# Key pages kept in two halves in HBM and fetched straight into the score operand, with a two-tensor normalisation

## The chip, the core and the metric

The program runs on one core of one Trainium2 chip. The metric is device time in microseconds (us), from one launch. TensorE (PE in the profile; its weight loads are PEld), VectorE (DVE), ScalarE (ACT), GpSimd (POOL) and SyncE (SP, which here only issues DMAs) run their own instruction streams and meet at semaphores.

## What is computed

A batch of 32 sequences with 32 tokens of 512 features goes through a grouped-query attention block with a paged key and value cache, and then through a dense layer with low-rank experts. Cut to what matters:

```python
q = rope(rmsnorm(x @ Wq.T)); k = rope(rmsnorm(x @ Wk.T)); v = x @ Wv.T      # 32 query heads, 8 key heads, D = 128
k_all = concat(k_cache[block_table], k); v_all = concat(v_cache[block_table], v)   # 16 pages of 32 tokens, + 32 own
scores = where(valid, q . k_all / sqrt(128), -1e30)
x = x + (softmax(scores) . v_all) @ Wo.T
x = x + x @ W.T + 2 * sum_e gate_e * (x @ A_e.T) @ B_e.T                      # top 2 of 8 experts
```

All inputs are float32. Scores and projections are computed in three passes: each operand is split into a high part (rounded to the type fp32r) and a low part (the rest), and hi·hi + hi·lo + lo·hi are summed in PSUM.

## The kernel before

**Tiling.** The eight key heads are taken two at a time: four groups g. In a group the 1024 token rows are eight tiles t of 128 rows (four sequences each), so there are 32 tiles, numbered i = 8g + t. A tile has eight pairs p: sequence b = p // 2 (four of them, ROWS) and key head h = p % 2. Tiles 1 to 5 of a group are one hardware loop, tiles 0, 6 and 7 are written out (walk, L55).

**One pair on each engine.** The orders are written by hand, as the bodies of PE (L632), ACT (L927), DVE (L1196), POOL (L1396) and SP (L419). Each engine takes its instructions in order and stops at each semaphore it waits for.

- PE at pair p: turn_probs(p) transposes the probabilities into PSUM (L576, L577); score(p+2) makes six matmuls of three passes into SX (L556); a piece of the projection of the next tile (proj, at p = 0 to 4); at p = 5 turn_q(i+1, 0) transposes the next queries; weigh(p) multiplies with the values into O (L590, L592). At p = 6 the score is the next tile's first one. project_out, 24 matmuls of 512 columns, starts at p = 7 before weigh(7) and ends the tile.
- DVE at pair p: normalise(p+1) (L1083), minimum(p+2) with the mask (L1076, reading SX), rest_kT(p+3) (L1096), then pieces of rope (rotate, L1052 to L1057), mean_square (L1064), and take_o(p) (L1092), the low part of O, which frees O for the next weigh (o_ready). At the end of a tile split_x (L1040, L1042) splits the input of the tile after the next, and add_y (L1117) adds the output.
- ACT at pair p: take_pT(p) (L842), take_kT(p+3) (L813), four squares with sums at p = 1, 3, 6 (L792), take_qT (L836), exponent(p+2) (L855), next_pages(p) (two DMA issues, L235), fill_slots (L829, the own keys of the tile behind the cached ones), take_block (L781 to L785, the projection out of PSUM), take_o_hi(p) (L849).
- POOL gathers the values of one sequence in four indirect DMAs (L1316), and does the sum, the power and the last product of rope (L1344, L1336, L1355) and the tables (L1331).
- SP issues twelve of the sixteen page fetches of each sequence (L350 to L352), the masks, weights and inputs.

**Pages.** The keys of a group are transposed in eight units of eight pages: PE turns 256 token rows into a PSUM bank (turn_unit, L529), ACT copies the bank to SBUF (take_unit, L761), SP stores it to kT_pages in HBM. Group 0 is turned at the start; the units of group g + 1 are turned during tiles 0 to 6 of group g: unit 0 at (t = 0, p = 2), unit t + 1 at p = 6 (unit_at, L224). A page is fetched as 128 rows of 256 bytes (two heads of 32 tokens, float32) into k_pages. take_kT and rest_kT then split one pair's 512 cached keys into kT, which has four slots; the split of a page is thus made again for every sequence that uses it, 256 times in all.

**Weights.** Each group's weights come in ten halves of 128x1024 through the two buffers of stage. ACT rounds a half (L861) and DVE takes the rest (L1016), at fixed places of tiles 6, 7 and 0 (HI_AT and LO_AT, L239). In tiles 1 to 5 stage is not used.

## Time and profile before

| | us |
|---|---|
| median of 3 runs (1472.35 to 1476.87) | 1476.8 |
| the profiled execution | 1477.62 |
| its span, first to last instruction | 1475.8 |
| start, up to the end of the first tile | 118.7 |
| 15 tiles t = 1 to 5 of groups 0 to 2 (three stretches) | 613.3 |
| 9 tiles t = 6, 7, 0 (three stretches) | 433.0 |
| 5 tiles t = 1 to 5 of group 3 | 193.0 |
| tile 6 of group 3 | 43.0 |
| last tile and the dense layer | 74.8 |

The stretches are bounded by the additions of y at the end of a tile (L1117). A row of the windows view gives for a stretch its length and, for each engine, the time in which it had an instruction running; the granted clock is TensorE's, 1.00 being 2.4 GHz and 0.50 being 1.2 GHz. In a timeline row the bracket is the time for which the engine had nothing to do before this instruction, and what released it. Transfers are 57% of the 16 DMA engines' time in the middle of the run, and 224.33 MB in all.

### The profile page before, as it was taken

The page shows a single profiled execution, that of the slowest core. Times are in us where ns is not written, and L with a number is a line of the kernel's source. Part 1 is how long each engine was busy: PE and PEld are TensorE (multiplying, and loading weights), DVE is VectorE, ACT ScalarE, POOL GpSimd, SP SyncE. Part 2 cuts the span into 40 slices and gives each one's busy share as a digit, 9 for nine tenths or more (in the row PEclk, how much of TensorE's full clock was granted, in tenths as well). Part 3 has the DMA queues.
Part 4 walks back from the last instruction along what each step waited for, and adds up shares of the span by engine and source line. Part 5 has one row for each costly group of instructions (what it writes and reads, how often), then busy time and mean ns, then how long its engine had stood idle before and what let it go on. Part 6 is the DMA issues. An engine that isn't in the chain of part 4 may idle for free. (4 is left out here: it accounts for less than half of the span.)

```text
span 1475.8 us, 34804 instructions
## 1 busy us (share of the span) xinstructions
PE 1255.9 (85%) x8000; PEld 1113.8 (75%) x8000; DVE 942.6 (64%) x2235; ACT 905.1 (61%) x2444; POOL 955.9 (65%) x1136
## 2 busy tenths in 40 slices
PE   4479899888788889889787999889878898999899
PEld 3368888777677778878676888788767787888787
DVE  5466666666756676676566666666676666676754
ACT  4366666666555666665556666666666666666651
POOL 5448776676556777677555876767666777777600
PEclk8689999999999999999999999999999999999999
DMA  8765565555656556555656655555565555555521
GB/s 250 201 171 158 152 154 156 138 153 145 180 155 168 138 148 157 141 154 150 165 139 182 163 145 154 146 146 155 146 178 154 155 142 143 147 140 138 140 77 57
DMA packets 393808, 224.33 MB, mean 152 GB/s; under 512 B 340882, under 2 KB 349362, under 8 KB 393524
## 3 DMA queue, kind: packets, MB, share of 16 engines
q1 hardware_dynamic: 294564, 136.76, 35.6%
q0 software_dynamic: 24576, 67.14, 15.2%
q10 hardware_dynamic: 74544, 19.10, 5.8%
q8 instruction: 38, 0.62, 0.2%
q14 instruction: 86, 0.70, 0.2%
HBM read 204.17 MB, written 20.75 MB: 152 GB/s over the span
## 5 line engine op out<-in xcount | busy, mean ns | idle before, releaser
L1316 POOL DMA_INDIRECT v_rows<-in_kv,step_idx x512 | 524.3, 1024 | 173.4 <-issue 138.3
L855 ACT ACTIVATE soft<-soft,min_all 128x544 f32<-128x544 f32 x256 | 191.6, 749 | 248.5 <-DVE min_all L1076 247.7
L590 PEld LDWEIGHTS O<-pT,v_rows 128*128 128x128 f32 x2048 | 277.8, 202 | 62.6 <-ACT pT L842 44.7
L590 PE MATMUL O<-pT,v_rows 128*128 128x128 f32 x2048 | 290.5, 288 | 38.6 <-DVE oT_lo L1092 27.5
L197 PE MATMUL SX<-kT,qT_hi 128*128 128x288 f32 (+1 forms) x1024 | 226.5, 310 | 56.2 <-ACT kT L829 33.1
L1076 DVE CUSTOM_DVE_ANT_0 soft<-SX,mask 128x544 f32<-128x544 f32 x256 | 183.6, 717 | 96.5 <-PE SX L197 96.2
L1092 DVE TENSOR_TENSOR oT_lo<-O,oT_hi 128x128 fp32r<-128x128 f32 x256 | 73.6, 288 | 241.6 <-ACT oT_hi L849 235.4
L197 PEld LDWEIGHTS SX<-kT,qT_hi 128*128 128x128 f32 x1024 | 164.4, 193 | 75.3 <-issue 51.7
L1336 POOL TENSOR_TENSOR rstd<-meansq,minus_half 128x4 f32<-128x4 f32 (+1 forms) x96 | 101.7, 1060 | 180.3 <-DVE meansq L1064 177.8
L842 ACT ACTIVATE pT<-PT 128x640 f32<-128x640 f32 x256 | 180.7, 706 | 20.7 <-PE PT L577 13.1
L1096 DVE TENSOR_TENSOR kT<-k_pages,kT 128x512 fp32r<-128x512 f32 x256 | 184.4, 721 | 7.0 <-ACT kT L813 3.6
L1083 DVE TENSOR_SCALAR soft<-soft,rden 128x544 f32<-128x544 f32 x256 | 182.8, 714 | 9.1
L197 PE MATMUL PROJ<-w_hi,x_hi 128*128 128x512 f32 x384 | 159.0, 414 | 34.4 <-ACT v_next L783 10.9
L576 PE MATMUL PT<-ident,soft 128*128 128x128 f32 x1024 | 159.2, 279 | 12.6 <-DVE soft L1083 10.7
L813 ACT ACTIVATE kT<-k_pages 128x512 fp32r<-128x512 f32 x256 | 161.9, 632 | 0.0
L197 PE MATMUL PROJ<-w_hi,x_lo 128*128 128x512 f32 x384 | 155.9, 406 | 0.0
L197 PE MATMUL PROJ<-w_lo,x_hi 128*128 128x512 f32 x384 | 154.2, 401 | 0.0
L197 PE MATMUL MISC<-wo_hi,oT_hi 128*128 128x512 f32 x256 | 108.9, 426 | 48.9 <-DVE oT_lo L1092 48.9
L197 PE MATMUL SX<-kT,qT_lo 128*128 128x288 f32 (+1 forms) x512 | 150.1, 293 | 0.0
L576 PEld LDWEIGHTS PT<-ident,soft 128*128 128x128 f32 x1024 | 123.9, 145 | 21.2 <-DVE soft L1083 14.2
L1344 POOL TENSOR_TENSOR rope_u<-rope_u,rope_v 128x512 f32<-128x512 f32 (+1 forms) x94 | 103.8, 1104 | 53.0 <-DVE rope_v L1057 50.7
L849 ACT ACTIVATE oT_hi<-O 128x128 fp32r<-128x128 f32 x256 | 69.6, 272 | 90.8 <-PE O L592 86.0
(222 smaller groups left out, 2382.9 us busy)
## 6 DMA issues: line engine op xcount, KB each, us to landing
k_pages<-kT_pages SPq DMA_DIRECT2D x1536, 32.0 KB
mask<-mask_rows SPq DMA_DIRECT2D x64, 272.0 KB, 3.6
k_pages<-kT_pages ACTq DMA_DIRECT2D x512, 32.0 KB
stage<-in_wqkv SPq DMA_DIRECT2D x22, 512.0 KB, 4.5
x_raw<-in_xT SPq DMA_DIRECT2D x32, 256.0 KB
v_rows<-in_kv,step_idx POOLq DMA_INDIRECT x512
stage<-in_wo SPq DMA_DIRECT2D x16, 512.0 KB, 5.7
y_tile<-y_running SPq DMA_DIRECT2D x32, 256.0 KB
```

Of the source, the lines that this page charges most:

```text
L197: mm = nc.tensor.matmul(out_ps, a, b, start=(c == 0 and k == 0), stop=(c == stop_at and k == 2))
L576: nc.tensor.transpose(PT[:, c * P:(c + 1) * P], probs[:, p % 2, c * P:(c + 1) * P], ident[:, :])
L590: nc.tensor.matmul(O[:, 0:P], v_rows[:, b, c, h * D:(h + 1) * D], pT[:, c * P:(c + 1) * P], start=c == 0, stop=False)
L813: nc.scalar.activation(kT[:, p % SLOTS, 0, 0:L].rearrange("p (j s) -> p j s", s=PSIZE), k_pages[:, b, :, h, :], ACT.Copy).then_inc(sm["kT_ ...
L842: nc.scalar.activation(pT[:, :], PT[:, 0:L + P], ACT.Copy).then_inc(sm["pT_ready"], 1)
L855: nc.scalar.activation(probs[:, p % 2, 0:KEYS], scores[:, p % 2, :], ACT.Exp, bias=min_all[:, p:p + 1], scale=-1.0, accum_out=den[:, p:p + ...
L1076: V.tensor_tensor_reduce(scores[:, p % 2, :], SX[:, SX_AT:SX_AT + KEYS], mask[:, b, :], 1.0, BIG, ALU.add, ALU.min, min_all[:, p:p + 1]).t ...
L1083: V.tensor_scalar(probs[:, p % 2, 0:KEYS], probs[:, p % 2, 0:KEYS], rden[:, p:p + 1], None, ALU.mult).then_inc(sm["probs_ready"], 1)
L1096: V.tensor_tensor(kT[:, p % SLOTS, 1, 0:L].rearrange("p (j s) -> p j s", s=PSIZE), k_pages[:, p // GK, :, p % GK, :], kT[:, p % SLOTS, 0, ...
L1316: G.indirect_dma_start(v_rows[:, b, c, :], None, v_half[:, :], bass.IndirectOffsetOnAxis(ap=step_idx[:, b * LC + c:b * LC + c + 1], axis=0 ...
L1336: G.tensor_tensor(rstd[:, 0:n], meansq[:, k, 0:n], minus_half[:, 0:n], ALU.pow).then_inc(sm["pow_ready"], 1)
L1344: G.tensor_tensor(rope_u[:, 0:w], rope_u[:, 0:w], rope_v[:, 0:w], ALU.add).then_inc(sm["sum_ready"], 1)
```

## The change

- A page in kT_pages is now 128 rows of 512 bytes: high parts of both heads, then low parts (PAGE_BYTES doubles). The split is made once for each unit: take_unit on ACT writes the high part, the new rest_unit on DVE the low part (32 times each), and the store writes both. take_kT and rest_kT (256 times each) are gone.
- kT holds all 16 pages of four sequences and the own keys behind them; a fetch writes into it directly. PE's score waits for the page DMAs (kp_in) where it waited for kT_ready, and a fetch into kT waits until the last score that reads those pages is done (s_done) where it waited for kT_ready. The moving operand of a score is now runs of 32 columns, 512 bytes apart; before it was 288 or 256 columns in one piece.
- The units of the next group are turned in tiles 1 to 4, two in each, at p = 2 and p = 6, in the stage buffers that the weights don't use then. The hardware loop (walk_tiles) is over tiles 1 to 4; tile 5 is written out. The first two halves of the next weights are loaded at tile 5.
- normalise multiplies by the broadcast reciprocal as a second tensor instead of a scalar operand, and mean_square takes its epsilon from a tensor.
- On ACT next_pages comes directly after take_pT, ahead of squares and exponential; take_unit comes after take_o_hi. On PE turn_q(i+1, 0) comes ahead of score at p = 5. On DVE split_x moves from the end of the tile to p = 6.
- At the start all eight units are turned before the first projection, their loads come first, and the first fetches of ACT stand later. The running y of the last layer lies in v_rows and q_rot.

The core of the diff:

```diff
-    PAGE_BYTES = D * GK * PSIZE * 4
+    PAGE_BYTES = D * 2 * GK * PSIZE * 4
     U8 = mybir.dt.uint8
-    kT_dram = nc.dram_tensor("kT_pages", (GROUPS * PAGES, D, GK * PSIZE), F32, kind="Internal").ap()
+    kT_dram = nc.dram_tensor("kT_pages", (GROUPS * PAGES, D, 2 * GK * PSIZE), F32, kind="Internal").ap()
...
-        k_pages = sb("k_pages", [P, ROWS, NPP, GK, PSIZE])
-        kn = sb("kn", [P, 2, GK * D])
+        kT = sb("kT", [P, ROWS, NPP + 1, 2, GK, PSIZE], F32R)
+        k_new = sb("k_new", [P, ROWS, 2, GK, SEQ], F32R)
...
-        kT = sb("kT", [P, SLOTS, 2, KEYS], F32R)
-        k_new = sb("k_new", [P, ROWS, GK, 2, SEQ], F32R)
...
+        kn = [stage[:, 0, k, :].rearrange("p (c n) -> p c n", c=2) for k in range(2)]
+
+        def unit_views(ps, dst):
+            src = ps.rearrange("p (h q s) -> p h q s", h=GK, q=UNIT_PAGES)
+            return src, [dst[:, :, z, :, :].rearrange("p q h s -> p h q s") for z in range(2)]
...
+        def unit_split(u, startup):
+            w = (wo_hi if u < 4 else wo_lo)[:, 2 * (u % 4):2 * (u % 4) + 2, :] if startup else stage[:, 1, :, :].bitcast(F32R)
+            return w.rearrange("p a n -> p (a n)").rearrange("p (q z h s) -> p q z h s", q=UNIT_PAGES, z=2, h=GK)
...
+        UNIT_AT = (2, 6)
...
+            return 2 * t - 2 + UNIT_AT.index(p)
...
-                sp.wait_ge(sm["kT_ready"], (i - 1) * PAIRS + b * GK + GK)
+                sp.wait_ge(sm["s_done"], (i - 1) * PAIRS + b * GK + GK)
...
+            def load_kn(n, g, u, k):
+
+                if k == 0:
+                    sp.wait_ge(sm["w_lo_ready"], g * HALVES)
+                    sp.nop(nofuse=True)
+                sp.wait_ge(sm["ku_done"], n - 1)
                 sp.nop(nofuse=True)
-                sp.dma_start(kn[:, :, :], kv[bass.ds(g * TOKENS_CACHED + u * (2 * P), 2 * P), 0:GK * D]
-                             .rearrange("(c p) n -> p c n", p=P)).then_inc(sm["kn_in"], 16)
+                sp.dma_start(kn[k], kv[bass.ds(g * TOKENS_CACHED + u * (2 * P), 2 * P), 0:GK * D]
+                             .rearrange("(c p) n -> p c n", p=P)).then_inc(kn_in[k], 16)
...
+            for c in range(4):
+                sp.dma_start(v_rows[:, c, :, :], kv[c * 4 * P:(c + 1) * 4 * P, 0:GK * D].rearrange("(c p) n -> p c n", p=P)
+                             ).then_inc(kn0_in[c], 16)
...
+                turning = not final and not fixed
...
+                if turning:
+                    for k in range(2):
+                        load_kn(n_unit + 2 * t - 2 + k, g + 1, 2 * t - 2 + k, k)
...
+                        sp.wait_ge(sm["ku_stored"], (g + 2) * 16 * UNITS)
+                        sp.nop(nofuse=True)
+                        next_half(g + 1, 0)
...
-                pe.wait_ge(sm["kT_ready"], n + 1)
+                if h == 0:
+                    pe.wait_ge(kp_in[b], (i + 1) * 16 * NPP)
...
-                    k_hi, k_lo = (kT[:, p % SLOTS, z, j0:j1] for z in range(2))
-                    mm = three_pass(SX[:, SX_AT + j0:SX_AT + j1], lambda c: (q_hi, q_lo), lambda c: (k_hi, k_lo), 1, 0, 0)
+                    k_hi, k_lo = (kT[:, b, j0:j1, z, h, :] for z in range(2))
+                    mm = three_pass(SX[:, SX_AT + j0 * SEQ:SX_AT + j1 * SEQ], lambda c: (q_hi, q_lo), lambda c: (k_hi, k_lo), 1, 0, 0)
...
+                    if not last and p == 5:
+                        turn_q(i + 1, 0)
...
-                    if not last and p == 5:
-                        turn_q(i + 1, 0)
...
-                nc.scalar.activation(unit_turned(u, startup).rearrange("p q h s -> p h q s"), unit_view(ps), ACT.Copy
-                                     ).then_inc(sm["ku_ready"], 1)
+                src, (hi, lo) = unit_views(ps, unit_split(u, startup))
+                nc.scalar.activation(hi, src, ACT.Copy).then_inc(sm["ku_hi"], 1)
...
-            def take_kT(i, p):
-                b, h = p // GK, p % GK
-                n = i * PAIRS + p
-                if h == 0:
-                    act.wait_ge(kp_in[b], (i + 1) * 16 * NPP)
-                if not (isinstance(n, int) and n < SLOTS):
-                    act.wait_ge(sm["min_ready"], CREDIT + n - SLOTS + 1)
-                nc.scalar.activation(kT[:, p % SLOTS, 0, 0:L].rearrange("p (j s) -> p j s", s=PSIZE), k_pages[:, b, :, h, :],
-                                     ACT.Copy).then_inc(sm["kT_hi_ready"], 1)
...
-                if not (isinstance(n, int) and n == 0):
-                    act.wait_ge(sm["s_done"], n)
-                nc.scalar.activation(kT[:, :, :, L:KEYS],
-                                     k_new[:, 2 * half:2 * half + 2, :, :, :].rearrange("p b h z s -> p (b h) z s"), ACT.Copy
+                if not (isinstance(i, int) and i == 0):
+                    act.wait_ge(sm["s_done"], (i - 1) * PAIRS + (half + 1) * (PAIRS // 2))
...
-                        act.wait_ge(sm["kT_ready"], i * PAIRS + p + GK)
+                        act.wait_ge(sm["s_done"], i * PAIRS + p + GK)
...
-                    if p + 3 < PAIRS:
-                        take_kT(i, p + 3)
-                    elif not last:
-                        take_kT(i + 1, p + 3 - PAIRS)
+                    if not last:
+                        next_pages(p)
...
-                    if not last:
-                        next_pages(p)
-                    u = unit_at(t, p)
-                    if u is not None and not final:
-                        take_unit(UNITS + g * UNITS + u, u, KT[:, :], False)
...
+                    u = unit_at(t, p)
+                    if u is not None and not final:
+                        take_unit(UNITS + g * UNITS + u, u, KT[:, :], False)
...
-                V.tensor_scalar(meansq[:, k, 0:n], sumsq[:, k, 0:n], 1.0 / D, EPS, ALU.mult, ALU.add
-                                ).then_inc(sm["ms_ready"], 1)
+                V.scalar_tensor_tensor(meansq[:, k, 0:n], sumsq[:, k, 0:n], 1.0 / D, eps[:, 0:n], ALU.mult, ALU.add
+                                       ).then_inc(sm["ms_ready"], 1)
...
-                V.tensor_scalar(probs[:, p % 2, 0:KEYS], probs[:, p % 2, 0:KEYS], rden[:, p:p + 1], None, ALU.mult
+                V.tensor_tensor(probs[:, p % 2, 0:KEYS], probs[:, p % 2, 0:KEYS], rden[:, p:p + 1].to_broadcast([P, KEYS]), ALU.mult
...
-            def rest_kT(i, p):
-                dve.wait_ge(sm["kT_hi_ready"], i * PAIRS + p + 1)
-                V.tensor_tensor(kT[:, p % SLOTS, 1, 0:L].rearrange("p (j s) -> p j s", s=PSIZE), k_pages[:, p // GK, :, p % GK, :],
-                                kT[:, p % SLOTS, 0, 0:L].rearrange("p (j s) -> p j s", s=PSIZE).bitcast(F32), ALU.subtract
-                                ).then_inc(sm["kT_ready"], 1)
+            def rest_unit(n, u, ps, startup):
+                dve.wait_ge(sm["ku_hi"], n + 1)
+                src, (hi, lo) = unit_views(ps, unit_split(u, startup))
+                V.tensor_tensor(lo, src, hi.bitcast(F32), ALU.subtract).then_inc(sm["ku_ready"], 1)
...
-                    if p + 3 < PAIRS:
-                        rest_kT(i, p + 3)
-                    elif not last:
-                        rest_kT(i + 1, p + 3 - PAIRS)
...
+                    u = unit_at(t, p)
+                    if u is not None and not final:
+                        rest_unit(UNITS + g * UNITS + u, u, KT[:, :], False)
...
+                        if not (final and fixed and t >= TILES - 2):
+                            split_x(i + 2)
...
-                if not (final and fixed and t >= TILES - 2):
-                    split_x(i + 2)
```

The order of instructions on ACT in the loop over tiles, pair 5. Before:

```order
L842 ACTIVATE pT<-PT 128x640
L810 REGISTER_ALU
L812 ISA
L813 ACTIVATE kT<-k_pages 128x512
L834 REGISTER_ALU
L836 ACTIVATE qT_hi<-MISC 128x4x4x32
L854 REGISTER_ALU
L855 ACTIVATE soft,den<-soft,min_all 128x544
L235 DMA k_pages<-kT_pages 128x256 x2
L829 ACTIVATE kT<-k_new 128x8x32
L849 ACTIVATE oT_hi<-O 128x4x32
```

Now:

```order
L858 ACTIVATE pT<-PT 128x640
L256 DMA kT<-kT_pages 128x512 x2
L850 REGISTER_ALU
L852 ACTIVATE qT_hi<-MISC 128x4x4x32
L870 REGISTER_ALU
L871 ACTIVATE soft,den<-soft,min_all 128x544
L845 ACTIVATE kT<-k_new 128x2x128
L865 ACTIVATE oT_hi<-O 128x4x32
```

The high part of the keys (L813 before) is gone, the two fetches stand directly behind pT, and the exponential is followed at once by the own keys (kT<-k_new) that the next score needs.

DVE in the same loop, from the minimum at pair 6 on. Before:

```order
L1076 ISA soft,min_all<-SX,mask 128x544
L1076 ISA min_all 128x1
L1095 REGISTER_ALU
L1096 TENSOR_TENSOR kT<-k_pages,kT 128x512
L1092 TENSOR_TENSOR oT_lo<-O,oT_hi 128x4x32
L1064 TENSOR_SCALAR meansq<-sumsq 128x4
L1081 RECIPROCAL rden<-den 128x1
L1083 TENSOR_SCALAR soft<-soft,rden 128x544
L1095 REGISTER_ALU
L1096 TENSOR_TENSOR kT<-k_pages,kT 128x512
L1092 TENSOR_TENSOR oT_lo<-O,oT_hi 128x4x32
```

Now:

```order
L1099 TENSOR_TENSOR oT_lo<-O,oT_hi 128x4x32
L1102 ISA
L1104 TENSOR_TENSOR stage<-KT,stage 128x2x8x32
L1071 SCALAR_TENSOR_TENSOR meansq<-sumsq,eps 128x4
L1044 ISA
L1046 REGISTER_ALU
L1047 CAST x_hi<-x_raw 128x512
L1049 TENSOR_TENSOR x_lo<-x_raw,x_hi 128x512
L1087 REGISTER_ALU
L1088 RECIPROCAL rden<-den 128x1
L1090 TENSOR_TENSOR soft<-soft,rden 128x544
L1099 TENSOR_TENSOR oT_lo<-O,oT_hi 128x4x32
```

The low part of the keys (L1096 before) is gone at both pairs; the low part of a unit (stage<-KT) and the split of x now stand between the low part of O and the next normalisation.

PE in the same loop, pair 5. Before:

```order
L576 MATMUL PT<-ident,soft 128x128 x4
L577 MATMUL PT<-ident,soft 128x128
L563 REGISTER_ALU
L197 MATMUL SX<-kT,qT_hi 128x288 x2
L197 MATMUL SX<-kT,qT_lo 128x288
L197 MATMUL SX<-kT,qT_hi 128x256 x2
L197 MATMUL SX<-kT,qT_lo 128x256
L550 MATMUL MISC<-ident,q_rot 128x128 x4
L590 MATMUL O<-pT,v_rows 128x128 x4
L592 MATMUL O<-pT,v_own 128x128
```

Now:

```order
L607 MATMUL PT<-ident,soft 128x128 x4
L608 MATMUL PT<-ident,soft 128x128
L580 MATMUL MISC<-ident,q_rot 128x128 x4
L596 REGISTER_ALU
L199 MATMUL SX<-kT,qT_hi 128x288 x2
L199 MATMUL SX<-kT,qT_lo 128x288
L199 MATMUL SX<-kT,qT_hi 128x256 x2
L199 MATMUL SX<-kT,qT_lo 128x256
L621 MATMUL O<-pT,v_rows 128x128 x4
L623 MATMUL O<-pT,v_own 128x128
```

The four transposes of the next queries have moved ahead of the six score matmuls.

## Rows read from the trace of the kernel before

**Rows 1.** The page: busy time and share of each engine.

```profile
PE 1255.9 (85%) x8000; PEld 1113.8 (75%) x8000; DVE 942.6 (64%) x2235; ACT 905.1 (61%) x2444; POOL 955.9 (65%) x1136
```

**Rows 2.** Windows: PE, PEld, DVE, ACT, POOL busy (instructions), granted clock, DMA share, GB/s.

```profile
0.00:118.70 118.70, 69.70 (x343) 58.38 (x344) 64.04 (x136) 57.33 (x140) 62.03 (x81) 0.83 0.74 205
118.70:323.00 204.30, 182.90 (x1212) 164.69 (x1211) 133.76 (x331) 133.32 (x370) 150.71 (x181) 0.97 0.57 149
323.00:469.00 146.00, 118.47 (x733) 103.13 (x732) 94.42 (x210) 88.56 (x233) 88.05 (x103) 0.95 0.61 163
469.00:674.00 205.00, 184.18 (x1209) 165.98 (x1208) 132.52 (x330) 132.87 (x370) 149.06 (x181) 0.97 0.57 148
674.00:821.00 147.00, 119.03 (x734) 103.76 (x733) 95.20 (x210) 88.93 (x233) 90.53 (x103) 0.94 0.60 162
821.00:1025.00 204.00, 183.91 (x1207) 165.31 (x1205) 131.03 (x330) 132.55 (x370) 146.65 (x179) 0.97 0.56 149
1025.00:1165.00 140.00, 116.36 (x722) 101.72 (x720) 94.66 (x209) 87.91 (x231) 89.35 (x102) 0.95 0.60 161
1165.00:1358.00 193.00, 175.17 (x1190) 158.26 (x1190) 131.41 (x331) 130.56 (x365) 147.03 (x176) 1.00 0.55 144
```

**Rows 3.** Lines L813, L1096, L1083, L765: duration ns min/median/max.

```profile
L813 ACT ACTIVATE kT<-k_pages x256: 613/630/657, 50.7 to 1413.9; 128x512 fp32r<-128x512 f32 x128
...
L1096 DVE TENSOR_TENSOR kT<-k_pages,kT x256: 678/686/2235, 51.6 to 1414.9; 128x512 fp32r<-128x512 f32 x128
...
L1083 DVE TENSOR_SCALAR soft<-soft,rden x256: 502/504/2133, 56.3 to 1419.2; 128x544 f32<-128x544 f32 x128
...
L765 ACT ACTIVATE kn<-KT x24: 597/597/598, 86.1 to 1060.0; 128x512 f32<-128x512 f32 x24
```

**Rows 4.** Waits of TensorE, whole span: us in total, times, longest.

```profile
PE MISC L197 <- DVE oT_lo L1092: 48.9, 28, 2.6
PE SX L197 <- ACT kT L829: 33.1, 34, 1.7
PE O L590 <- DVE oT_lo L1092: 27.5, 26, 1.5
```

**Rows 5.** Timeline of one tile of the last group: start us, us, what [idle before].

```profile
1265.43 1.13 PE L590 MATMUL O<-pT,v_rows 128*128 128x128 f32 x8 [0.69 <-DVE oT_lo L1092]
...
1267.77 0.42 ACT L829 ACTIVATE kT<-k_new 128x256 fp32r<-128x256 f32 x1 [0.35 <-issue]
...
1268.53 0.50 PE L197 MATMUL SX<-kT,qT_hi 128*128 128x288 f32 x2 [1.19 <-ACT kT L829]
...
1268.78 1.39 DVE L1083 TENSOR_SCALAR soft<-soft,rden 128x544 f32<-128x544 f32 x1
...
1271.89 0.28 ACT L849 ACTIVATE oT_hi<-O 128x128 fp32r<-128x128 f32 x1 [0.21 <-issue]
...
1272.64 0.47 PE L197 MATMUL MISC<-wo_hi,oT_hi 128*128 128x512 f32 x1 [1.47 <-DVE oT_lo L1092]
```

**Rows 6.** Timeline of TensorE at the same place, tile of another group.

```profile
1014.99 0.47 PE L197 MATMUL MISC<-wo_hi,oT_hi 128*128 128x512 f32 x1 [2.36 <-DVE oT_lo L1092]
...
1016.08 0.63 PE L197 MATMUL MISC<-wo_lo,oT_hi 128*128 128x512 f32 x1
```

**Rows 7.** Timeline around a group boundary.

```profile
721.05 0.49 PE L197 MATMUL PROJ<-w_hi,x_hi 128*128 128x512 f32 x1 [2.72 <-DVE x_lo L1042]
...
749.13 2.13 DVE L1083 TENSOR_SCALAR soft<-soft,rden 128x544 f32<-128x544 f32 x1
```

**Rows 8.** The page: DMA queues, packets, MB, share of 16 engines.

```profile
q0 software_dynamic: 24576, 67.14, 15.2%
q10 hardware_dynamic: 74544, 19.10, 5.8%
```

**Rows 9.** Timeline of the start.

```profile
48.91 0.60 ACT L785 ACTIVATE raw<-PROJ 128x512 f32<-128x512 f32 x1 [6.22 <-issue]
...
52.58 0.82 PE L197 MATMUL SX<-kT,qT_hi 128*128 128x288 f32 x2 [10.52 <-DVE kT L1096]
```

154 lines of the change are left out of this document (73 added, 81 removed).

## The prediction

> **What bounds the kernel now.** I read the page first: TensorE has a matmul running for 85% of the span, VectorE, ScalarE and GpSimd for 61 to 65% [rows 1]. So TensorE sets the time, together with whatever makes it wait, and the next question is where it waits. I cut the span at the ends of tiles [rows 2]. In the last group five tiles take 193.0 us, 38.6 each, at full clock. In the other groups five such tiles take 204 to 205, 41 each, at a granted clock of 0.97. Three tiles around a group boundary, where the weights are split, take 140 to 147, 48 each, at 0.94 to 0.95: TensorE is busy for 119.0 of 147.0 us there. The start takes 118.7.
>
> The list of TensorE's waits names the handovers: for the low part of O on VectorE before project_out (48.9 us, 28 times) and before weigh (27.5), for the own keys from ScalarE (33.1) [rows 4]. None is long by itself. In one tile of the last group they are three gaps [rows 5]: A, 0.69 us before weigh(5); B, 1.19 before the next tile's first score; C, 1.47 before project_out. That is 3.35 us, so the tile without gaps would take 38.6 - 3.35 = 35.3 us. In the other groups gap C is 2.36 us, since a unit's copy (0.6 us) stands ahead of the high part of O, and behind it matmuls of 512 columns take 0.63 instead of 0.39 to 0.40: the granted clock has gone from 2.4 to 1.2 GHz [rows 2, 6].
>
> All three gaps end a chain that runs over both ScalarE and VectorE, each of which works through a fixed order. What is taken out of these orders shortens the chain; what is taken out elsewhere is worth nothing.
>
> **Part 1: the split of pages.** It removes 256 x 0.63 = 161 us from ScalarE and 256 x 0.72 = 184 from VectorE (the median there is 0.686) [rows 3], and adds 32 copies of about 0.6 and 32 differences of about 0.69: net 142 and 162 us. None of it is TensorE's, so it counts only through the gaps. For a tile without a unit:
>
> - Gap A waits for take_o(4), behind rope's last block, behind ScalarE's copy of it. Both engines lose one key half ahead of it (0.63 and 0.69), and the copy no longer stands behind two fetches (0.35 us of issue time, as before the own keys in rows 5). TensorE comes there about 0.5 later, as turn_q now lies in front. Gap A goes: 0.69.
> - Gap B waits for fill_slots behind exponent(7). By the same chain it starts about 1.0 earlier, but TensorE comes 0.69 earlier. Net 0.3 gained: about 0.9 stays.
> - Gap C waits for take_o(6), at the end of pT, two fetches, four squares and the exponential on ScalarE. 0.63 goes, but the exponential needs minimum(0) of the next tile, which stands behind a normalisation that took 1.39 us [rows 5]. I take half of it: net 0.3 gained, 1.2 stays.
>
> Together 1.3 us a tile. Five tiles of the last group: 6.5 us.
>
> **Part 2: units in tiles 1 to 4.** Two units a tile where there was one. Each costs TensorE four transposes, at most 4 x 1.13 / 8 = 0.56 us; I take 0.5. The one at p = 6 falls into gap B and costs nothing, the one at p = 2 costs 0.5. ScalarE's copy now comes behind the high part of O, so gap C is that of the last group and I expect the clock to stay at 2.4 GHz as it did there. VectorE's difference (0.69) now stands before mean_square at p = 6; GpSimd's power and product come after that, and turn_q(i+1, 1) needs them: I take 0.6 for it (between nothing, if rope's chain has slack, and 1.2, if x's split in front of the next normalisation counts too). A tile is then 38.6 - 1.3 + 0.5 + 0.6 = 38.4, and tile 5, without units, 37.3. Twelve and three of these are 460.8 + 111.9 = 572.7 us against 613.3 [rows 2]: 40.6 us.
>
> **Part 3: group boundaries.** TensorE idles for 28 of 147 us there; three tiles without weights idle for 3 x 3.5 = 11 [rows 2], so 17 are the boundary's. The split of x moves from behind a weight half to p = 6, and its wait of 2.72 us [rows 7] goes. Three units leave (1.5 us of transposes). A clock of 0.94 on 147 us is up to 8.8 us lost; I give back 3 with the long wait. Of the other 14 us idle I take half, 7, since the engines that split weights lose 15 and 17 of their 89 and 95 us. 14.2 us a boundary, 42.6 for three. The last group's tile 6 and last tile: 2.5 together, by the same share.
>
> **Part 4: normalisation.** Its median is 504 ns, but its longest 2133 [rows 3, 7]; its mean is 714. The nearest row for the new form is L1096, also a product of two SBUF tensors: 686 ns at 512 columns, so 729 at 544, with a longest of 2235. In total nothing changes (729 against 714 x 256), if the stalls go; if they all stay, 210 ns each, VectorE gains 58 us of work. I take a third of them. The Trainium skill, "SBUF — State Buffer", section "SBUF: two separate sides", says that a VectorE operation with two SBUF inputs still takes the port pair it shares with GpSimd, but only against a GpSimd operation that reads SBUF. By that rule stalls behind gathers would end and those behind rope's sums (1.39 us in rows 5 is one, with L1344 beside it in the trace) would stay, which speaks against a full gain; the sum above already leaves gap C for that.
>
> **Part 5: transfers.** A page row grows from 256 to 512 bytes, 2048 x 128 = 262,144 packets. A packet of ScalarE's queue, 256 bytes, takes 5.8% x 16 x 1475.8 / 74,544 = 18.4 ns, one of GpSimd's, 2732 bytes on average, 146 [rows 8]. On a line between them 512 bytes take 31.6. The extra is between nothing and 18.4 ns a packet, or 0 to 301 us of all 16 engines; I take 13.1 ns, 215 us. The DMA share goes from 0.57 to about 0.75: busy, not full. Fetches start up to seven pairs ahead, so in the loop I cost this at nothing; what it costs if that cover is gone is rival 4. ("DMA: Bandwidth & Descriptors" in the Trainium skill, section "Specifications", names 512 bytes as the least transfer for line rate; by that rule the extra would be near nothing. No row here has such packets in number.)
>
> **Part 6: the start.** The third projection's copy stood 6.22 us behind fetches, and the first score waited 10.52 us [rows 9]. Both now come earlier; then twelve fetches (some 6.5 us) stand before the first exponential instead. I take 7 us off, for the first scores and for the page list that all wait for. The bound on the other side: 64 fetches and 8 stores, 16,384 packets, are 13.4 us more of all engines at 13.1 ns, at a share of 0.74 already [rows 2]; not hidden, the start is 6 us longer than now.
>
> **The sum.** 6.5 + 40.6 + 42.6 + 2.5 + 7 = 99.2 us. From the profiled execution, 1477.6 (span 1475.8), this gives 1378.4; the median of the three runs is 0.8 lower, so 1378.
>
> **Rivals.**
>
> 1. *The chains fall wholly behind TensorE.* For: only 3.35 us a tile is idle, and both engines lose a fifth of their work. Against: squares, exponential and own keys still follow each other within 3.8 us. A further 2.1 us in 20 tiles and 7 at each boundary: 1378 - 63 = 1315.
> 2. *The two-input product stalls as the old one did.* VectorE carries 58 us more, at the pairs where the chain runs. Then B and C keep their length (-12), units cost a further 1 us in twelve tiles (-12), and boundaries gain half (-21): 1378 + 45 = 1423.
> 3. *TensorE reads 32-column runs more slowly: slower than before.* No moving operand of the old trace was in pieces. A pair's scores are 3 x 544 = 1632 columns, 0.68 us at 2.4 GHz; at half rate 256 pairs add 174 us, all on TensorE: 1552. It turns the result from 57% longer on (99 of 174). Against: the copies of ScalarE and VectorE read such pieces without a loss (L813, 630 ns for 512 columns, against 597 for L765) [rows 3].
> 4. *Pages come late.* The score now waits for the DMA itself, two pairs later than the split did, but nothing buffers it. SP issues twelve fetches in 6 us, and the last sequence's pages can only be asked for after pair 7's score. At 2 us a tile: 1378 + 64 = 1442; from 3.1 us a tile on nothing is gained.
>
> That the new order does not do what it says (fetches ahead of the exponential cost ScalarE the same 0.35 us, only elsewhere) lies within the forecast, since squares follow them directly at three pairs.
>
> **Chances.** Forecast (1350 to 1410) 0.55; rival 1 0.17; rival 2 0.15; rival 3 0.06; rival 4 0.07. The range 1320 to 1440 leaves out rival 3, a third of rival 1 and half of rival 4, some 0.16. A measurement of this kernel tells 0.3% from no change. Faster by more than that 0.91, the same 0.02 (the far end of rival 4), slower 0.07.
>
> **What would show it.** Tiles 1 to 5 of the last group at 37.3 us each, with gap A gone, B near 0.9 and C near 1.2; the same tiles of other groups at 38.4 with the clock at 1.00; the boundary stretches at 130; score matmuls of 256 and 288 columns as long as before; no wait of the scores for kT_pages; normalisations at about 729 ns with a few above 1.2 us; a DMA share of 0.65 to 0.8. The prediction is wrong if scores wait for DMAs, if the boundaries keep their 145 us, or if GpSimd, whose gathers and rope work fill 147 of 193 us [rows 2] and leave little room, becomes what TensorE waits for.

## The result and the profile after

The changed kernel takes 1431.1 us (median of 4 runs, 1428.3 to 1434.3) against 1476.8: a ratio of 0.970, 95% interval 0.967 to 0.973. It is faster by 46 us; 99 were forecast. The profiled execution took 1432.97 us, its span is 1431.1. Between the two profiled spans TensorE's idle time fell by 18 us (span less busy time, 219.9 to 201.5) and its busy time by 26 (1255.9 to 1229.6, the same 8000 matmuls, at a granted clock of 0.973 instead of 0.957).

The busy line of the page, the granted clock and the DMA share of the changed kernel:

```profile
PE 1229.6 (86%) x8000; PEld 1091.1 (76%) x8000; DVE 837.2 (58%) x2012; ACT 770.8 (54%) x2188; POOL 956.4 (67%) x1136
...
PEclk8689999999999999999999999999999999999999
DMA  8877777777767777877767777777777676777711
```

Against [rows 1], ScalarE and VectorE have lost work, as the change meant; TensorE's share has hardly risen. The windows view, bounded by the ends of tiles as in [rows 2]: length, busy us of each engine, granted clock, DMA share and GB/s.

```profile
0.00:118.00 118.00, 66.26 (x331) 55.00 (x332) 60.95 (x134) 49.30 (x125) 60.64 (x80) 0.80 0.78 240
118.00:318.70 200.70, 181.13 (x1225) 162.45 (x1224) 121.44 (x299) 113.70 (x334) 146.77 (x177) 1.00 0.78 222
318.70:455.00 136.30, 113.77 (x716) 99.86 (x715) 79.11 (x184) 73.98 (x206) 92.75 (x105) 0.96 0.73 210
...
656.60:791.70 135.10, 110.88 (x716) 97.41 (x715) 79.81 (x185) 73.51 (x206) 93.64 (x107) 0.97 0.73 211
...
992.10:1124.10 132.00, 111.63 (x717) 98.35 (x716) 80.08 (x185) 73.89 (x206) 94.45 (x107) 0.97 0.74 216
1124.10:1312.10 188.00, 175.92 (x1192) 158.88 (x1191) 113.84 (x290) 111.10 (x326) 143.22 (x177) 1.00 0.73 204
```

Put beside the forecast (spans, us; "four waits gone" is run e17 below):

| stretch | before | forecast | changed | four waits gone |
|---|---|---|---|---|
| start and first tile | 118.7 | 111.7 | 118.0 | 106.3 |
| 15 tiles t = 1 to 5, groups 0 to 2 | 613.3 | 572.7 | 602.7 | 582.0 |
| 9 tiles t = 6, 7, 0 | 433.0 | 390.4 | 403.4 | 376.7 |
| 5 tiles t = 1 to 5, group 3 | 193.0 | 186.5 | 188.0 | 185.6 |
| the rest | 117.8 | 115.3 | 119.0 | 116.6 |

The last group came out nearly as forecast. The missing time lies in the start (6 us), the 15 tiles of groups 0 to 2 (30), the boundaries (13) and the rest (4). TensorE's waits in the changed kernel (total us, times, longest) name the places; the answer to [rows 4]:

```profile
PE MISC L199 <- DVE oT_lo L1099: 37.0, 32, 1.3
PE SX L199 <- ACT kT L845: 27.9, 35, 1.1
PE O L621 <- ACT pT L858: 26.2, 13, 5.2
PE PROJ L580 <- POOL q_rot L1360: 13.9, 20, 0.9
PE PROJ L199 <- ACT raw L811: 11.9, 5, 10.4
...
PE PROJ L199 <- ACT v_next L809: 10.7, 2, 9.9
...
PE KT L563 <- DMA stage<-in_kv: 7.5, 7, 2.2
```

The first two are the old gaps C and B. The other five are new or grown, each with one place in an order behind it (v_next had 10.9 us before too, but its longest was 4.8). Four of them (the probabilities pT, the queries q_rot, v_next and KT) are taken away in e17; the one for raw, 10.4 us in the start, is not touched by any experiment.

**The start.** Timeline of the changed kernel, first tile:

```profile
67.52 0.85 SPq L332 DMA_DIRECT2D stage<-in_wo  x2
...
68.54 6.54 SPq L256 DMA_DIRECT2D kT<-kT_pages  x12
...
75.13 0.31 SPq L358 DMA_DIRECT2D pages<-page_bytes  x1
...
78.75 0.87 ACTq L256 DMA_DIRECT2D kT<-kT_pages  x2
...
79.73 0.75 ACT L871 ACTIVATE soft<-soft,min_all 128x544 f32<-128x544 f32 x1 [14.68 <-issue]
...
81.24 0.79 PE L199 MATMUL PROJ<-w_hi,x_hi 128*128 128x512 f32 x1 [9.86 <-ACT v_next L809]
```

ScalarE's next fetches need the second tile's page list (pages), which SP loads behind all 48 fetches of the first tile. They stood behind the exponential before; now the exponential stands behind them, for 14.68 us, and TensorE waits 9.86 for what follows it.

Earlier in the start stands the wait for raw, in the same timeline:

```profile
33.84 0.85 SPq L332 DMA_DIRECT2D stage<-in_wqkv  x2
...
37.91 1.06 ACT L904 ACTIVATE w_hi<-stage 128x1024 fp32r<-128x1024 f32 x1 [10.68 <-DMA stage<-in_wqkv]
...
40.73 0.79 PE L199 MATMUL PROJ<-w_hi,x_hi 128*128 128x512 f32 x1 [10.39 <-ACT raw L811]
...
53.12 0.82 PE L199 MATMUL SX<-kT,qT_hi 128*128 128x288 f32 x2 [5.88 <-DMA kT<-kT_pages]
```

SP issues these two weight halves behind the stores of the units, at 33.84 us; before, it issued them at 25.36, and the same wait of TensorE was 3.39 us. So the first score comes at 53.12 us, no earlier than before (52.58 in [rows 9]).

**Tile 7.** Timeline of the changed kernel, group 1, pairs 2 and 3:

```profile
710.90 4.15 SPq L256 DMA_DIRECT2D kT<-kT_pages  x7
...
715.37 0.33 SPq L332 DMA_DIRECT2D stage<-in_wqkv  x1
...
720.39 1.06 ACT L877 ACTIVATE w_hi<-stage 128x1024 fp32r<-128x1024 f32 x1 [7.81 <-DMA stage<-in_wqkv]
...
721.35 0.69 ACT L858 ACTIVATE pT<-PT 128x640 f32<-128x640 f32 x1
722.09 1.23 PE L621 MATMUL O<-pT,v_rows 128*128 128x128 f32 x4 [5.20 <-ACT pT L858]
```

SP issues the weight half behind twelve page fetches, as in the kernel before. But by the records ScalarE now comes to it 12.6 us after the addition that ends the last tile (before, 15.5), and SP issues it after 15.4 (14.1 and 14.3 in the other two groups; before, 12.6 to 13.0). ScalarE stands 7.81 us at it, and TensorE waits 5.20 for the probabilities behind it. The three boundaries have such a wait each, 4.8 us in the mean.

**Pair 6 of a tile with a unit**, timeline of the changed kernel (group 2, t = 1):

```profile
862.60 0.29 DVE L1099 TENSOR_TENSOR oT_lo<-O,oT_hi 128x128 fp32r<-128x128 f32 x1 [1.07 <-ACT oT_hi L865]
...
863.09 0.69 DVE L1104 TENSOR_TENSOR stage<-KT,stage 128x512 fp32r<-128x512 f32 x1 [0.20 <-ACT stage L792]
863.69 0.15 DVE L1071 SCALAR_TENSOR_TENSOR meansq<-sumsq,eps 128x4 f32<-128x4 f32 x1
...
863.93 1.16 POOL L1341 TENSOR_TENSOR rstd<-meansq,minus_half 128x4 f32<-128x4 f32 x1 [3.63 <-DVE meansq L1071]
...
865.22 1.42 POOL L1360 TENSOR_TENSOR q_rot<-rope_u,rstd 128x512 f32<-128x512 f32 x1
...
866.69 0.55 PE L580 MATMUL PROJ<-ident,q_rot 128*128 128x128 f32 x3 [0.92 <-POOL q_rot L1360]
```

The mean square (0.15 us of work) waits behind the unit's copy on ScalarE and difference on VectorE; GpSimd has been idle for 3.63 us, and TensorE for 0.92 us before it turns the queries.

### The profile page after: what moved, and what is told of

Read it like the earlier page. It is cut to its first block and busy times, and to the rows that moved or that the text cites. A ratio compares the mean times of both kernels' runs of the same rounds, so it can differ in the third digit from the quotient of the medians.

```text
span 1431.1 us, 33847 instructions
## 1 busy us (share of the span) xinstructions
PE 1229.6 (86%) x8000; PEld 1091.1 (76%) x8000; DVE 837.2 (58%) x2012; ACT 770.8 (54%) x2188; POOL 956.4 (67%) x1136
## 3 DMA queue, kind: packets, MB, share of 16 engines
q10 hardware_dynamic: 74544, 35.88, 8.9%
## 5 line engine op out<-in xcount | busy, mean ns | idle before, releaser
L621 PE MATMUL O<-pT,v_rows 128*128 128x128 f32 x2048 | 279.0, 280 | 38.3 <-ACT pT L858 26.2
L621 PEld LDWEIGHTS O<-pT,v_rows 128*128 128x128 f32 x2048 | 264.8, 194 | 61.1 <-ACT pT L858 36.1
L1083 DVE CUSTOM_DVE_ANT_0 soft<-SX,mask 128x544 f32<-128x544 f32 x256 | 183.8, 718 | 93.4 <-PE SX L199 92.5
L1090 DVE TENSOR_TENSOR soft<-soft,rden 128x544 f32<-128x544 f32 x256 | 230.9, 902 | 8.8
L199 PE MATMUL PROJ<-w_hi,x_hi 128*128 128x512 f32 x384 | 155.8, 406 | 31.0 <-ACT raw L811 11.9
L199 PE MATMUL MISC<-wo_hi,oT_hi 128*128 128x512 f32 x256 | 105.4, 412 | 37.0 <-DVE oT_lo L1099 37.0
L1349 POOL TENSOR_TENSOR rope_u<-rope_u,rope_v 128x512 f32<-128x512 f32 (+1 forms) x94 | 107.9, 1148 | 21.9 <-DVE rope_v L1064 20.0
L1059 DVE TENSOR_TENSOR rope_u<-raw,table 128x512 f32<-128x512 f32 (+1 forms) x96 | 57.9, 603 | 100.0 <-ACT raw L811 65.7
L199 PEld LDWEIGHTS PROJ<-w_hi,x_hi 128*128 128x128 f32 x384 | 74.5, 194 | 45.6 <-issue 15.7
```

Source lines behind the costliest of these rows:

```text
L199: mm = nc.tensor.matmul(out_ps, a, b, start=(c == 0 and k == 0), stop=(c == stop_at and k == 2))
L621: nc.tensor.matmul(O[:, 0:P], v_rows[:, b, c, h * D:(h + 1) * D], pT[:, c * P:(c + 1) * P], start=c == 0, stop=False)
L1083: V.tensor_tensor_reduce(scores[:, p % 2, :], SX[:, SX_AT:SX_AT + KEYS], mask[:, b, :], 1.0, BIG, ALU.add, ALU.min, min_all[:, p:p + 1]).t ...
L1090: V.tensor_tensor(probs[:, p % 2, 0:KEYS], probs[:, p % 2, 0:KEYS], rden[:, p:p + 1].to_broadcast([P, KEYS]), ALU.mult).then_inc(sm["probs ...
L1349: G.tensor_tensor(rope_u[:, 0:w], rope_u[:, 0:w], rope_v[:, 0:w], ALU.add).then_inc(sm["sum_ready"], 1)
```

## The experiments

e1 to e8, e17 and e18 are told against 1431; the kernel before, which ran beside each, took 1475 to 1477 us there. In the sessions of e9 to e16 it took 1560 to 1562 us, with VectorE and ScalarE idle for reasons that the trace doesn't name, so these are compared with each other only. An interval behind a time is that of the ratio to the kernel before.

**e1: the page list early, at the start.**

```diff
+                if b == 2:
+                    sp.wait_ge(sm["pages_read"], 1)
+                    sp.nop(nofuse=True)
+                    load_list(1)
                 for j in range(SP_PAGES):
                     fetch_page(sp, b, j, page[b % 2 * SP_PAGES + j])
...
-            sp.wait_ge(sm["pages_read"], 1)
-            load_list(1)
```

> At the start SyncE loads the second tile's page list before it issues the fetches of the third and fourth sequence, not after them. Theory (a few new order slots ate the gain): the 9.9 us for which TensorE waits in the first tile, while ScalarE holds its next exponential back for the list, go almost wholly: 8 to 10 us off the changed kernel, 1422. The first tile ends at 109 instead of 118 us. Rival (the start is bound by transfers, at a DMA share of 0.78): the wait moves to the pages of sequences 2 and 3, gain under 3 us, 1429.

Measured 1429.3 (ratio 0.963 to 0.971): 2 us, too little to tell from nothing (four runs of 1428.6 to 1430.2 against 1428.3 to 1434.3). The wait of 9.9 us is gone from the trace, but later in the first tile stands one of 6.9, "PE O <- ACT pT": the next in the order of the same queue, a weight half behind twelve page fetches, at which ScalarE stands 7.0 us. The theory named the wait rightly and its worth wrongly; the rival's time fits, its reason doesn't (see e3).

**e2: the weight half ahead of the fetches, in tile 7.**

```diff
+                if ending:
+                    next_half(g + 1, 5)
                 if not last:
                     read_pages(i + 1, 0)
                     load_pages(i + 1, 0)
...
-                if ending:
-                    next_half(g + 1, 5)
```

> In the last tile of groups 0 to 2 SyncE issues the sixth weight half ahead of the first twelve page fetches, not behind them. Theory (order): the half is issued 9 us earlier and has landed when ScalarE comes to it; TensorE's wait of 4.8 us before weigh(3) goes in three tiles: 14 us off, 1417, boundary stretches at 128 to 131. Rival (512-byte packets fill the queues, so that what is issued also lands later): the half's transfer grows and the pages of sequence 0 come late instead, gain under 5 us, 1427.

Measured 1415.3 (0.954 to 0.963): 16 us, where the theory said 14. The first boundary stretch of it, in the windows view:

```profile
315.90:445.90 130.00, 111.36 (x716) 98.44 (x715) 79.36 (x184) 73.72 (x206) 91.30 (x106) 0.97 0.75 220
```

**e3: half the bytes.** A fetch takes `[:, 0:GK * PSIZE * 4]` of each row, 256 bytes, and k_lo is read from the high part, so the low part of the keys is left out of the result.

> A fetch takes only the high parts, 256 bytes a row, and the score uses the high part of the keys twice, so the low part of the keys is left out of the result; matmuls, orders and packet counts stay. The share of the DMA engines falls to that of the kernel before. Theory (bytes are hidden, order slots are not): the waits for the page list (9.9) and for the weight half (4.8 a boundary) stay within 1 us; only the wait for the unit's rows (0.84 in 9 tiles) shrinks: 1420 to 1430. Rival (bytes): waits for transfers go everywhere, 1390 to 1405.

Measured 1425.2 (0.961 to 0.969): 6 us for 67 MB less, at the edge of the noise (the changed kernel's interval is 0.967 to 0.973). Averaged from the records, the start's wait goes from 9.9 to 7.5 us, tile 7's from 4.8 to 3.7, that for a unit's rows from 0.84 to 0.79. So the bytes lengthen these waits a little, the order makes them.

**e4: the scalar normalisation**, in the changed kernel.

```diff
-                V.tensor_tensor(probs[:, p % 2, 0:KEYS], probs[:, p % 2, 0:KEYS], rden[:, p:p + 1].to_broadcast([P, KEYS]), ALU.mult
+                V.tensor_scalar(probs[:, p % 2, 0:KEYS], probs[:, p % 2, 0:KEYS], rden[:, p:p + 1], None, ALU.mult
```

> Only the normalisation goes back to the scalar operand. Theory: its median falls from 725 to 504 ns and its mean from 902 to about 720, 47 us less of VectorE, of which gaps B and C give 0.2 us each a tile: 10 us off, 1421. Rival (the chain through VectorE is what keeps the gaps): 0.7 us and more a tile, 1405 or less. Second rival (the scalar form blocks GpSimd, which now works 67% of the time and has TensorE waiting for q_rot): no gain or slower, 1430 to 1438.

Measured 1412.4 (0.953 to 0.961): 19 us off, between the theory's 10 and the rival's 26. **e5** is the mirror, the tensor form in the kernel before:

> The kernel before, with only the normalisation by a second tensor. Theory (the new form costs VectorE 0.2 us a normalisation, and stalls behind rope's sums as the old one did): the mirror of what undoing it gave in the changed kernel (19 us): 1477 + 10 to 19 = 1487 to 1496. Rival (it paid in the kernel before, where 22 normalisations stalled beside gathers, and costs only since the orders changed): 1470 to 1477.

Measured 1502.4, 1.018 (1.016 to 1.021) of the kernel before: 27 us slower than the kernel before beside it, past the theory's range. Durations (minimum/median/longest, ns) of the normalisation in the changed kernel, in e4 and in e5:

```profile
L1090 DVE TENSOR_TENSOR soft<-soft,rden x256: 724/725/2491, 57.1 to 1374.7; 128x544 f32<-128x544 f32 x128
```

```profile
L1090 DVE TENSOR_SCALAR soft<-soft,rden x256: 502/504/2166, 56.5 to 1352.5; 128x544 f32<-128x544 f32 x128
```

```profile
L1083 DVE TENSOR_TENSOR soft<-soft,rden x256: 724/726/2415, 57.7 to 1443.0; 128x544 f32<-128x544 f32 x128
```

The median rises by 0.22 us and the longest stay. In both kernels this part of the change cost time. In e5 the clock hid some of it; windows view, the first five tiles and those of the last group:

```profile
121.70:326.50 204.80, 179.93 (x1212) 160.52 (x1211) 145.84 (x332) 133.13 (x370) 153.88 (x176) 1.00 0.58 149
1179.10:1379.70 200.60, 177.58 (x1192) 158.17 (x1191) 144.90 (x331) 130.25 (x366) 153.06 (x176) 1.00 0.55 138
```

The last group takes 200.6 instead of 193.0 [rows 2], 1.5 us a tile. The first stretch takes 204.8, as before, but at a clock of 1.00 instead of 0.97: gap C is 2.0 us there instead of 2.3 (averages from the records), and the matmuls behind it run at 2.4 GHz (in the 15 tiles 2 of project_out's 360 take over 550 ns, in the kernel before 38).

**e6: mean_square ahead of take_o and rest_unit** at pair 6.

```diff
+                    if not last and p == 6:
+                        mean_square(i + 1, 2)
                     take_o(i, p)
...
-                        mean_square(i + 1, 2)
```

> In the changed kernel mean_square of pair 6 stands ahead of take_o and rest_unit on VectorE. Theory (in the tiles with units GpSimd's power and product wait behind the copy, the low part of O and the unit's difference): TensorE's 0.92 us before turn_q(i+1, 1) go in 12 tiles and 0.3 in others: 12 to 15 us off, 1417; unit tiles 39.8. Rival (the squares of ScalarE end no earlier, and VectorE now waits for them ahead of the low part of O): nothing gained, gap C grows, 1431 to 1436.

Measured 1408.2 (0.953 to 0.959): 23 us, more than the theory's 15. "PE PROJ <- POOL q_rot" (13.9 us, 20 times) is no longer among the waits of TensorE. Five tiles of the first group, in its windows view:

```profile
114.20:310.00 195.80, 179.82 (x1225) 162.40 (x1224) 118.80 (x299) 113.38 (x334) 144.05 (x176) 1.00 0.80 226
```

195.8 instead of 200.7. By the records tiles 2 to 4 gain 0.9 us each, tile 1 0.7 and tile 5 1.5, where a wait for q_rot before MISC goes too. The wait for a unit's rows grows meanwhile, from 0.84 to 1.27 in tiles 2 to 4.

**e7: own keys and the high part of O ahead of the exponential** (ScalarE, pairs 5 and 6).

```diff
+                    if not last and p == 5:
+                        fill_slots(i + 1, 0)
+                    if p == 6:
+                        take_o_hi(i, p)
                     if p + 2 < PAIRS:
                         exponent(i, p + 2)
...
-                    if not last and p == 5:
-                        fill_slots(i + 1, 0)
...
-                    take_o_hi(i, p)
+                    if p != 6:
+                        take_o_hi(i, p)
```

> In the changed kernel ScalarE takes the own keys (pair 5) and the high part of O (pair 6) ahead of the exponential, in the 0.6 and 0.9 us in which it waits for the minimum. Theory (gaps B and C are places in ScalarE's order, not its load): B falls from 0.89 to under 0.3 and C from 1.30 to about 0.5, some 1.2 us a tile in 29 tiles: 35 us off, 1396. Rival (VectorE's and GpSimd's part of the chain ends at the same time): under 0.4 us a tile, 1420.

Measured 1413.2 (0.955 to 0.959): 18 us, half of the theory's 35. Gaps B and C fall to 0.2 us and less, as the theory said or further, and in tiles with units too. In the last group a tile gains 1.2 us, but in tiles with units nothing: there TensorE's wait for q_rot grows from 0.9 to 1.6 and that for the unit's rows from 0.84 to 1.25. By the stretches 10 of the 18 us come from the boundaries and 6 from the last group. A gap is worth what the next chain leaves.

**e8: all of it together**: e1, e2, e4, e6, e7 and the two further edits that stand at e17.

> The changed kernel with all of it: page list early, the weight halves of tiles 7 and 0 ahead of page fetches, mean_square early, the rows of the units asked for first in a tile, the scalar normalisation, own keys and high part of O ahead of the exponential. Theory (each wait was its own): 19 + 8 + 18 + 12 + 10 + 35 = 102 us off 1431, 1329, with 5 to 15 us given back where one wait hid another: 1329 to 1344. Rival (the gain of each was another's cover): over 1375.

Measured 1357.2 (0.916 to 0.922): 74 us off, between theory and rival, the fastest kernel of this study. Alone e4 and e7 gave 19 and 18 us; added to e17 (below) they give 13 together. Its busy line:

```profile
PE 1227.7 (90%) x8000; PEld 1090.3 (80%) x8000; DVE 791.0 (58%) x2012; ACT 770.8 (57%) x2188; POOL 913.9 (67%) x1136
```

**e17: the four new waits taken away, nothing else.** It is e1, e2 and e6, the weight halves of tile 0 in the same way, and the units' rows asked for first in a tile; normalisation and ScalarE's order stay as changed. What it adds to e1, e2 and e6:

```diff
+                if turning:
+                    for k in range(2):
+                        load_kn(n_unit + 2 * t - 2 + k, g + 1, 2 * t - 2 + k, k)
                 if not (final and fixed and t >= TILES - 2):
                     load_x(i + 2, (t + 2) % TILES if fixed else t + 2)
...
-                if turning:
-                    for k in range(2):
-                        load_kn(n_unit + 2 * t - 2 + k, g + 1, 2 * t - 2 + k, k)
...
+                if ending:
+                    next_half(g + 1, 5)
+                if fixed and t == 0:
+                    next_half(g, WO_FIRST + 2)
                 if not last:
                     read_pages(i + 1, 0)
                     load_pages(i + 1, 0)
                 if fixed and t == 0:
-                    next_half(g, WO_FIRST + 2)
-                if ending:
-                    next_half(g + 1, 5)
+                    next_half(g, WO_FIRST + 3)
```

> The kernel of e11 and e14, the changed kernel without its four new waits. Theory: 55 us off 1431, 1376 to 1384, a ratio of 0.932 to 0.937 to the kernel before. Rival (a chain through VectorE with the slower normalisation takes the place of each wait): 1395 or more, 0.945.

Measured 1370.3 (0.924 to 0.932): 61 us off the changed kernel. Its stretches, windows view:

```profile
0.00:106.30 106.30, 63.41 (x330) 52.96 (x331) 61.23 (x133) 49.78 (x125) 61.98 (x84) 0.87 0.86 264
106.30:300.70 194.40, 180.10 (x1225) 162.53 (x1223) 122.73 (x298) 114.02 (x334) 143.61 (x176) 1.00 0.80 231
300.70:428.30 127.60, 109.63 (x716) 96.73 (x715) 81.36 (x184) 73.72 (x206) 89.93 (x107) 0.99 0.77 224
1049.40:1235.00 185.60, 173.64 (x1185) 158.07 (x1185) 117.58 (x293) 112.69 (x328) 143.62 (x176) 1.00 0.73 207
```

Alone e1, e2 and e6 give 2 + 16 + 23 = 41 us, so 20 come from the two further edits and from taking the waits away together; no run tells these apart. Against the profiled execution of the changed kernel TensorE's idle time falls by 44 us (201.5 to 157.4) and its busy time by 20 (1229.6 to 1209.9), at a granted clock of 0.988 instead of 0.973. What e8 gains beyond e17 its boundaries give back in part: by the records the 15 tiles fall from 582.0 to 569.1 us and the last five from 185.6 to 180.8, but the three boundaries rise from 376.7 to 385.5, at a clock of 0.95, 0.99 and 0.95 where e17 has 0.99, 0.99 and 1.00.

**e18: e8_all with the page list ahead of the fetches of sequence 2** in every tile.

```diff
                     read_pages(i + 1, 1)
+                    if not (final and fixed and t == TILES - 2):
+                        sp.wait_ge(sm["pages_read"], i + 2)
+                        sp.nop(nofuse=True)
+                        load_list(i + 2)
                     load_pages(i + 1, 2)
...
                     load_pages(i + 1, 3)
-                    if not (final and fixed and t == TILES - 2):
-                        sp.wait_ge(sm["pages_read"], i + 2)
-                        sp.nop(nofuse=True)
-                        load_list(i + 2)
```

> The kernel of e8_all with one edit: in every tile SyncE loads the next page list ahead of the fetches of sequence 2, not behind those of sequence 3. Theory (ScalarE stands up to 5 us at the page list at pair 0, TensorE 0.9 us at pair 1 in tiles 2 to 4 and 2.6 in tile 7): 16 off 1357, 1338 to 1346, a ratio of 0.91. Rival (the wait moves to the gathers of GpSimd or to the weights): 1352 or more.

Measured 1368.5 (0.924 to 0.930), 11 us slower than e8_all: the rival. ScalarE's idle "issue" time before exponentials falls from 92.9 to 6.8 us, so the list was what it waited for, and TensorE's waits for v_next fall from 22.9 to 1.7; but ScalarE's waits for weight halves rise from 8.5 to 30.1 us, and TensorE's for pT from 11.2 to 34.3 and for a unit's rows from 8.3 to 14.5. Why these transfers land later isn't settled.

**e9 to e16, the other sessions.** VectorE's waits in the changed kernel there (e13):

```profile
DVE oT_lo L1099 <- ACT oT_hi L865: 202.0, 160, 14.6
DVE soft L1083 <- remote: 125.0, 54, 4.1
DVE oT_lo L1099 <- issue: 63.0, 25, 4.7
```

The minimum (soft, L1083) waits 125 us for a releaser that is not in this core's trace; in the traces of the kernel before, the changed kernel, e6, e8 and e17 there is no wait with such a releaser. Two sessions, e9 to e12 in one and e13 to e16 in the other, agree within 0.5% on the kernels that both had.

> In the changed kernel the two fetches of a pair go back behind the exponential on ScalarE, as in the kernel before. Theory (in the loop ScalarE idles 0.6 to 0.9 us ahead of the exponential, so the order of the two is worth nothing there; only the first tile waits for its page list, and behind that wait stands one for a weight half): 1427 to 1431. Rival 1 (the own keys come 0.35 us later a tile, behind the issue): 1436 to 1441. Rival 2 (the fetches ahead of the exponential are what holds the chain): under 1420.

e9 puts `next_pages(p)` back behind `exponent` on ScalarE. It took 1585.6, 1.016 of the kernel before, where the changed kernel (e13) has 0.977. e9 and e13 ran in different sessions, so this is a comparison of ratios: fetches ahead of exponentials are worth 4% there, the direction of rival 1 and several times its size. What they are worth where the kernel before takes 1476 wasn't run.

> The changed kernel without the 24 units of tiles 1 to 4: no rows loaded, nothing turned, split or stored, and groups 1 to 3 fetch the keys of group 0, so the keys of groups 1 to 3 are left out of the result; fetches keep their number and size. Theory (two units cost a tile 1.36 us of TensorE, 0.84 of waiting for rows and 0.92 for the rotated queries): tiles 2 to 4 fall from 40.7 to 37.6 us as in the last group, twelve tiles give 33 to 37 us: 1394 to 1398. Rival (groups 0 to 2 are slower for another reason, for instance weights or clock): under 20 us, 1411 or more.

In e10 `unit_at` returns None, `turning` is False, and the page lists of all groups have the offsets of group 0, so the keys of groups 1 to 3 are left out of the result. It gave 1495.7; its repeat e15 1496.5 beside 1525.2 for the changed kernel (e13).

> The changed kernel itself, as the foot of the next three on the same chip: 1431, or 0.970 of the kernel before. If the chip is like that of e9 to e12 (the kernel before at 1560), both theories expect the same 4 to 8 per cent on all of the four.

> The kernel of e10: the changed kernel without the units of tiles 1 to 4, groups 1 to 3 fetching the keys of group 0, so that the keys of groups 1 to 3 are left out of the result. Theory (two units cost a tile 1.36 us of TensorE, 0.84 of waiting for rows and 0.92 for the rotated queries): tiles 2 to 4 fall from 40.7 to 37.6 us: 1394 to 1398. Rival (groups 0 to 2 are slower for another reason): under 20 us off, 1411 or more.

29 us, between theory and rival. Tiles t = 1 to 5 of group 0 in e13 and in e15:

```profile
117.90:338.40 220.50, 188.71 (x1228) 165.97 (x1227) 113.59 (x299) 113.29 (x334) 145.85 (x178) 0.98 0.73 204
```

```profile
117.50:329.80 212.30, 184.92 (x1195) 163.95 (x1193) 107.92 (x291) 109.15 (x325) 144.42 (x178) 0.98 0.65 182
```

8.2 us for eight units in this stretch, 3.8 of it TensorE's busy time. By the records the stretches of groups 1 and 2 give 12.8 and 11.4, and tiles 2 to 4 fall by 2.6 us each where 3.1 was expected.

> The changed kernel with its four new waits taken away, and nothing else: page list early, weight halves of tiles 7 and 0 ahead of page fetches, the rows of a unit asked for first in its tile, mean_square of pair 6 early. The normalisation and ScalarE's order stay as changed. Theory (these waits are what the forecast of 1378 missed): 9 + 18 + 5 + 23 = 55 us off, 1376 to 1384. Rival (without the scalar normalisation the chain through VectorE takes the place of each wait): 1395 or more.

e11 gave 1470.2, its repeat e14 1463.8, 61 us off e13 of its own session: the size that e17 then showed.

> The kernel of e11: the changed kernel with its four new waits taken away and nothing else. Theory (these waits are what the forecast of 1378 missed): 9 + 18 + 5 + 23 = 55 us off the changed kernel, 1376 to 1384. Rival (a chain through VectorE with the slower normalisation takes the place of each wait): 1395 or more.

> The kernel of e8_all with two more: in every tile the next page list is loaded ahead of the fetches of sequence 2, and the first unit of a tile is turned at pair 3. Theory (ScalarE at pair 0 stands up to 5.1 us at the page list, so that TensorE waits 0.9 us in a unit tile and 2.6 in tile 7; the rows of the first unit come 0.9 late): 9 x 1.8 + 3 x 2.6 = 24 off 1357, 1333 to 1340. Rival (GpSimd with its gathers, 67% busy, ends next): over 1350.

> The kernel of e12: e8_all with the next page list ahead of the fetches of sequence 2 in every tile, and the first unit of a tile at pair 3. Theory (ScalarE stands up to 5.1 us at the page list at pair 0, and the rows of the first unit come 0.9 late): 24 off the 1357 of e8_all, 1333 to 1340. Rival (the page list was not what it waited for, or GpSimd ends next): 1350 or more.

Both are e18 with `UNIT_AT = (3, 6)`. e12 gave 1505.4 and e16 1502.7, slower than the kernel with four edits in the same sessions (1470 and 1464), a miss of the theory. The list, which loses 11 us in e18, may be part of it; what the rest is stays open.

## Why the prediction was wrong, and where it was right

**The step that failed, in one sentence.** The sum had no term for what SP's and VectorE's orders deliver late once TensorE comes earlier (the second unit "costs nothing", boundary idle time halved in bulk, 7 us off the start); in its place four waits stood, and taking them away gave 61 us (e17). The parts in turn:

**Part 1, right.** A tile of the last group takes 188.0 / 5 = 37.6 us; 37.3 was forecast. Gap A is gone but for 0.2 us, gap B went from 1.26 to 0.89 (averages over five tiles, from the records). Gap C hardly moved (1.34 to 1.30): the high part of O still stands behind the exponential, that behind the minimum, and that behind a normalisation of 1.57 us. e7, which changes that order, takes it away. With C and most of B still there, rival 1 is out; both engines were to lose a sixth of their work (142 of 905 us and 162 of 943), not the fifth that it says. ScalarE lost 134 us and VectorE 105; of the 57 that VectorE kept beyond the forecast 48 are the normalisation of part 4.

**Part 2, the first step that failed.** Forecast 38.4 us, measured 40.7 in tiles 2 to 4, and 38.8 in tile 5, which has no unit, where 37.3 was forecast. The clock is right: 1.00 in the first stretch, and no tile has the slow matmuls of [rows 6]. Four terms were low. The base is 37.6, not 37.3. The transposes of two units take TensorE 1.36 us (tile less gaps, 36.56 against 35.20 in the last group), where I had 0.5: I costed the one at pair 6 at nothing, "falls into gap B", but of that gap (0.89) 0.51 stays, so it hid 0.38 of its 0.68 and the two cost 1.0 in all. The wait for q_rot is 0.92, not 0.6. And the rows of the tile's first unit, 0.84 us late, were not in the sum: their load stands on SP behind the storing of the last unit and of y. These four make 1.9 of the 2.3 us; the rest is in shorter waits. e6 takes the wait for q_rot away, and tiles 2 to 4 are at 39.8; e17 takes both away, and they are at 39.2.

**Part 3, the second step that failed.** Tiles 6 and 0 gave 3.6 and 5.5 us each, but tile 7 only 0.4, since a new wait of 4.8 replaced what it had lost. Over the three boundaries TensorE's idle time fell by 12.0 us ([rows 2] and the windows above: 79.1 to 67.1), where the sum has 3 x (2.7 + 7) = 29; its busy time fell by 17.6, where the sum has 3 x (1.5 + 3) = 13.5. So the term for the clock and the units held, and the one for idle time did not. I had counted it in bulk ("half of 14") and not asked what SP's queue delivers when. e2 takes the wait away: 16 us. In e17 boundaries take 126 us each where 130 was forecast.

**Part 4, a term put at nothing that measured 19 us, so rival 2 was partly true.** I called it "in total nothing changes" and took a third of the stalls to stay, without a term for them. They stayed (54 of 256 normalisations are over 1.3 times the median; before, 60), the mean went from 714 to 902 ns, and e4 shows 19 us. Which GpSimd work stalls them is worked out from the records. In the changed kernel 100 normalisations overlap one of rope's sums (L1349) or last products (L1360): 54 of these are stretched, and the mean of the 100 is 1164 ns. Another 92 overlap a gather and none of these: not one is stretched, the longest takes 729 ns. e5 agrees: 50 of 77, and none of 78. By the rule of the Trainium skill ("SBUF — State Buffer", section "SBUF: two separate sides") the stalls beside gathers would end and those beside rope's sums stay: the trace agrees with both. But there was little to end: in the kernel before 53 of the 60 stretched ones already overlapped rope's sum or product, and only 7 of the 77 beside a gather alone were stretched, to 0.75 us at most. I had taken two thirds of all stalls to end. That 1431 lies near rival 2's 1423 is luck: the normalisation is 19 of its 45 us, and e17 gets to 1370 with the normalisation as changed.

**Part 5, right.** No score waits for pages after the first tile, and reading 32-column runs costs nothing: SX matmuls take 313 ns in the mean, before 310, so rival 3 is out. ScalarE's queue shows the packet price:

```profile
q1 hardware_dynamic: 294564, 195.48, 47.2%
...
q10 hardware_dynamic: 74544, 35.88, 8.9%
```

8.9% x 16 x 1431.1 / 74,544 = 27.3 ns a packet, against 31.6 forecast and 18.4 before (65,536 of these packets are rows of pages). The extra, 8.9 ns, is neither the 13.1 that I took nor near nothing. (215 us on a share of 0.57 make 0.72 and not 0.75; the trace has 0.73 to 0.78 behind the start.) Bytes in all are worth 6 us (e3), so rival 4 holds little.

**Part 6, the third step that failed.** I took 7 us off "for the first scores and for the page list that all wait for", and said that the first scores come earlier. They come at 53.12 us, before at 52.58: the third projection's copy no longer stands behind fetches, but two weight halves now stand behind the units' stores, and TensorE waits 10.39 us for them instead of 3.39. The fetches ahead of the first exponential I priced at their issue time; what they waited for was the list, 14.7 us. e1 shows that behind it stood a further wait; only together (e17) do they give 12 us. What the wait of 10.39 us is worth wasn't run.

**The sum.** The four waits that SP's and VectorE's orders made cost 61 us (e17), more than the 53 that the forecast missed. Without them the kernel is at 1370, below the 1378 forecast, and the scalar normalisation and ScalarE's other order take it to 1357 (e8). So the mechanism was right (what leaves the two orders shortens the chains behind TensorE), and the error was to look at the chains that were there and not at the entries of a queue that become late when TensorE comes earlier, or when the entry ahead is allowed to block. Of the 46 us gained no run tells apart what the split of pages, the units in tiles 1 to 4 and the moves of turn_q and split_x gave.

## What to carry to other kernels

Before you move an instruction ahead of another, ask what it can wait for, and not what it costs: two fetches that take 0.87 us to issue held an exponential for 14.7. When the main engine gets faster, go through each DMA queue for the entries that were just in time, and order them by who needs them first. And price each part of a change alone: here one part (the normalisation, 19 us) took back two fifths of what the whole gained. Then measure the parts together, since their prices don't add: 19 and 18 us alone (e4, e7) were 13 us on top of e17.

## What the hardware showed

- A multiplication of two SBUF tensors on VectorE, 128x544, takes 0.725 us against 0.504 for tensor by scalar. Where it overlaps rope's sum or last product on GpSimd the first takes 1.16 us in the mean (100 times, changed kernel, 54 stretched), the second 0.97 (103 times, e4, 58 stretched). Beside a gather alone the first was never stretched (170 times in the changed kernel and e5), the second 8 times of 162 (kernel before and e4), to 0.75 us at most.
- On ScalarE's queue, whose packets are mostly rows of pages, fetches of 64 KB in 512-byte rows take 27 ns a packet where those in 256-byte rows take 18: twice the bytes for half as much again of engine time.
- The same kernel (the one before) on the same chip number took 1475 us in one session and 1562 in another. The changed kernel's trace has waits of VectorE there whose releaser isn't in it. In such a session edits are worth other sums: e8_all with two more edits stood behind the kernel with four.
